# Routing in the attention phase: logits with the gate stationary, transposed back for two batches, and a table of steps for the choice and the places

## The chip, the cores and the metric

The kernel runs on one core of one Trainium2 chip. Time is device microseconds of one execution. The profile is one more execution, with the span of its records and its own time.

## What is computed

32 batches of 256 tokens, width 256, go through cross attention with 16 heads, and then through a mixture of 16 experts of which each token uses four. Of the reference, what matters here:

```python
x = x + xattn(layernorm(x), ctx_1024, ctx_1024, mask, Wq, Wk, Wv, Wo, 16)
# the experts, on layernorm(x):
scores = sigmoid(xt @ gate_w.T)                  # 16 logits a token
_, idx = top_k(scores + gate_b, 4)
w = take_along_axis(scores, idx, axis=-1)
w = w / sum(w, axis=-1, keepdims=True) * 2.5
# y = sum over the four experts of w * expert(xt), plus a shared expert
x = x + y
```

## The kernel before

There are two phases, attention (`emit_attention`) and the experts (`expert_phase`). Attention is one long list of steps, written out for each engine and joined by semaphores. A step `g` is one head of one batch: `b, h = divmod(g, H)` with H = 16, so 512 steps, and a tail to step 520 in which the last pieces end. "Step 6" below means h = 6 in some batch. In every step TensorE makes the scores of head g (L888, L889), a projection of K or Q into one of two `pj` banks (L85 to L87), transposes the probabilities of head g - 3 (L899) and multiplies those of head g - 4 by V (L912). VectorE adds the mask and finds the maximum (L1130), inverts the sums (L1105), adds the halves of the values (L1140; the upper 64 partitions in one step, the lower in the next), writes the low part of Q or K (L1097) and of the probabilities (L1149). float32 products are made of high and low parts, three matmuls each.

Other work shares the `pj` banks at fixed steps: V at steps 4, 5, 12, 13; the output projection at 14, 0, 6, 8; the transposes of x at 9 and of the normed rows at 2 (`rT`). The dictionary `uses` lists what fills a bank in which step. TensorE waits in `bank` until VectorE has emptied the use two before (`s_pjfree`), and every engine takes its part in the order of its own program. So work of VectorE that stands ahead of a low part holds up the bank two uses later.

Routing lies between. For batch b - 2, in step 7, `lg` makes the logits: the transposed rows `xrT` (high and low part) are stationary, the gate with its high and low half is the moving operand of 32 columns, eight matmuls for two tiles of 128 tokens (L837). VectorE sums the halves into `r_sc` (L1064). A set is two batches. In the 15 steps behind the second one's logits `Router.choose` runs one piece k a step: k = 0, 1 the sigmoid (L225, L229), 2 the bias (L231), 3 and 4 the largest values (L235), 5 and 6 their indices (L239), 7 a cast (L242), 8 the one-hot (L244), 9 and 10 halves and mask (L248, L250), 11 the product of one-hot and scores and its reduce (L253, L256), 12 to 14 the weights. A set's pieces thus begin in step 9 of an odd batch and end in step 7 of the next. Three groups of 14, 10 and 8 batches have their rows sorted by expert. For the first two, TensorE counts ranks (`rk`, step 10 of batches 16 and 26, L271 to L278), and `Router.place` turns them into places in the next 18 or 16 steps, with a product and a reduce (L327, L331) for every four tiles. GpSimd then scatters rows by indirect DMA, one every 1.5 steps. It also scales the probabilities (L792) and makes the low parts of the attention (L741) and of the context, the latter in step 3 (L736).

```python
    SET_FROM = [(SET_BATCHES * s + SET_BATCHES + 1) * H + LG_STEP + 1 for s in range(SETS - 1)]
```

```python
                for t, start in enumerate(SET_FROM):
                    if start < g <= start + router.SET_STEPS:
                        router.choose(dve, t, g - start - 1)
```

## Time and profile before

| what | value |
|---|---|
| median of 3 runs | 2213.93 us (2211.66 to 2216.16) |
| the profiled execution's own time | 2211.4 us |
| its span | 2209.6 us |
| ScalarE and GpSimd busy, share of the span | 76% and 63% |
| HBM traffic over the span | 129 GB/s |

Busy time is a sum over instructions; the windows below cut it into stretches. TensorE's records overlap, so in attention a busy share near 100% can still hide waits of about 0.1 us; the start of one matmul to the start of the next shows them. The batches of attention do the same matmuls, apart from logits and ranks, so their lengths can be compared.

### The profile page before, as it was taken

The numbers are of one execution on the slowest core, as the hardware profiler recorded it, in microseconds if no ns is written. First come the engines' busy times: TensorE is split into PE (matmuls) and PEld (weight loads), VectorE is DVE, ScalarE is ACT, GpSimd is POOL, SyncE is SP. The second block draws the span as 40 slices with busy tenths as digits, with TensorE's granted clock in tenths as the row PEclk, the third lists the DMA queues.
The fourth block names the chain that finished last, engine by engine and source line by source line (L and its number), as shares of the span: only waits on it lengthen the run. The fifth ranks groups of instructions, "written<-read, shape, count | busy, mean of one in ns | idle before, by whom it ended". The sixth has DMA issues, their size and how long they took to land. (4 is left out here: it accounts for less than half of the span.)

```text
span 2209.6 us, 57976 instructions
## 1 busy us (share of the span) xinstructions
PE 2086.8 (94%) x16512; PEld 2006.3 (91%) x16512; DVE 1865.4 (84%) x6129; ACT 1677.5 (76%) x4795; POOL 1400.1 (63%) x2094
## 2 busy tenths in 40 slices
PE   7999999999999999999999999999899998898885
PEld 6999999999999998999999998999799998888884
DVE  7999999999999999999999999999764446666687
ACT  6989889888888888898898888889655554454531
POOL 4555655555555555888778877876656646656665
PEclk9999999999999999999999999999999999999997
DMA  7777767777777766866666666666678768887897
GB/s 207 188 182 191 187 175 187 184 181 192 179 187 184 182 168 169 220 188 171 176 180 174 176 167 162 177 172 167 217 254 277 266 240 283 274 283 269 268 331 242
DMA packets 262128, 457.32 MB, mean 207 GB/s; under 512 B 36544, under 2 KB 148672, under 8 KB 261824
## 3 DMA queue, kind: packets, MB, share of 16 engines
q1 hardware_dynamic: 237248, 386.48, 62.8%
q0 software_dynamic: 24576, 67.14, 9.5%
q8 instruction: 148, 2.42, 0.4%
q14 instruction: 156, 1.28, 0.2%
HBM read 141.00 MB, written 144.70 MB: 129 GB/s over the span
## 5 line engine op out<-in xcount | busy, mean ns | idle before, releaser
L792 POOL TENSOR_SCALAR E<-E,rinv 128x256 f32<-128x256 f32 x1024 | 479.6, 479 | 474.8 <-DVE rinv L1105 470.0
L980 ACT ACTIVATE E<-E,negmax 128x256 f32<-128x256 f32 x1024 | 508.9, 502 | 6.8 <-DVE negmax L1130 6.6
L1130 DVE CUSTOM_DVE_ANT_0 E<-pS,m_in 128x256 f32<-128x256 f32 x1024 | 387.5, 416 | 34.4 <-PE pS L889 30.9
L1149 DVE TENSOR_TENSOR PT_lo<-pT,PT_hi 128x512 fp32r<-128x512 f32 x512 | 350.6, 685 | 27.7 <-ACT PT_hi L998 23.6
L1602 POOL DMA_INDIRECT block<-expert_rows,slot x256 | 247.0, 965 | 168.5 <-remote 69.9
L998 ACT ACTIVATE PT_hi<-pT 128x512 fp32r<-128x512 f32 x512 | 304.9, 596 | 9.7 <-PE pT L899 0.5
L899 PE MATMUL pT<-ident,E 128*128 128x128 f32 x2048 | 306.6, 272 | 0.4 <-POOL E L792 0.4
L912 PE MATMUL pV<-PT_hi,V 128*128 128x256 f32 x1024 | 287.2, 303 | 6.1 <-DVE PT_lo L1149 6.0
L964 ACT ACTIVATE qk_sp<-pj 128x256 fp32r<-128x256 f32 x512 | 196.4, 384 | 109.1 <-PE pj L87 95.7
L888 PE MATMUL pS<-qk_st 128*128 128x256 f32 x1024 | 269.1, 284 | 7.8 <-DMA qk_st<-qk_sp 7.6
L889 PE MATMUL pS<-qk_st,qk_sp 128*128 128x256 f32 x1024 | 266.4, 282 | 0.0
L912 PE MATMUL pV<-PT_lo,V 128*128 128x256 f32 x1024 | 265.4, 281 | 0.0
L899 PEld LDWEIGHTS pT<-ident,E 128*128 128x128 f32 x2048 | 235.9, 141 | 0.8 <-POOL E L792 0.6
L1097 DVE TENSOR_TENSOR qk_sp<-pj,qk_sp 128x256 fp32r<-128x256 f32 x512 | 215.0, 420 | 10.6 <-ACT qk_sp L964 2.7
L1140 DVE TENSOR_TENSOR att_sum<-pV,att_sum 64x256 f32<-64x256 f32 x512 | 211.4, 413 | 11.2 <-ACT att_sum L989 1.9
L741 POOL TENSOR_TENSOR att_lo<-att_sum,att_hi 128x256 fp32r<-128x256 f32 x256 | 192.4, 751 | 24.2 <-ACT att_hi L1007 20.5
L912 PEld LDWEIGHTS pV<-PT_hi,V 128*128 128x128 f32 x1024 | 193.9, 189 | 14.3 <-DVE PT_lo L1149 8.6
L989 ACT ACTIVATE att_sum<-pV 64x256 f32<-64x256 f32 x512 | 193.8, 379 | 16.4 <-PE pV L912 4.1
L888 PEld LDWEIGHTS pS<-qk_st 128*128 128x128 f32 x1024 | 195.5, 191 | 10.1 <-DMA qk_st<-qk_sp 9.8
L912 PEld LDWEIGHTS pV<-PT_lo,V 128*128 128x128 f32 x1024 | 194.6, 190 | 6.1
L980 ACT ACTIVATION_READ_ACCUMULATOR E<-E,negmax 128x1 f32 x1024 | 197.9, 193 | 0.0
L889 PEld LDWEIGHTS pS<-qk_st,qk_sp 128*128 128x128 f32 x1024 | 195.7, 191 | 0.1
(265 smaller groups left out, 6879.3 us busy)
## 6 DMA issues: line engine op xcount, KB each, us to landing
qk_st<-qk_sp SPq DMA_DIRECT2D x512, 192.0 KB
qk_st<-qk_sp SPq DMA_DIRECT2D x512, 128.0 KB
sorted_rows<-qk_st SPq DMA_DIRECT2D x152, 256.0 KB, 3.5
xg<-sorted_rows SPq DMA_DIRECT2D x76, 512.0 KB
expert_rows<-block SPq DMA_DIRECT2D x76, 512.0 KB
acc<-x_plus_attention SPq DMA_DIRECT2D x35, 256.0 KB
x_in<-in_x SPq DMA_DIRECT2D x32, 256.0 KB
c_in<-in_ctxT SPq DMA_DIRECT2D x32, 256.0 KB, 4.0
```

The source lines that it names most:

```text
L792: last = pool.tensor_scalar(e[:, t, :], e[:, t, :], rinv[:, r, t:t + 1], 1.0, ALU.mult, ALU.mult)
L888: pe.matmul(pS[g % 2][:, t, :], stacked[:, a, Q_HI, at], stacked[:, a, K_HI, :], start=True, stop=False)
L889: last = pe.matmul(pS[g % 2][:, t, :], plain[:, Q_HI, at], stacked[:, a, K_LO, :], start=False, stop=True)
L899: last = pe.transpose(pT[g % 2][:, k, t * P:(t + 1) * P], e[:, t, k * P:(k + 1) * P], ident[:, :])
L912: last = pe.matmul(pV[g % 2][:, 0:S], V[:, k, j, 2 * a:2 * a + 2, :], PT[g % PT_RING][part][:, k, :], start=k + part == 0, stop=k == NT - ...
L980: last = act.activation(E[r][:, t, :], E[r][:, t, :], ACT.Exp, bias=negmax[:, r, t:t + 1], scale=-1.0, accum_out=rowsum[:, r, t:t + 1])
L998: act.activation(PT[m % PT_RING][0][:, :, :], pT[m % 2][:, :, :], ACT.Copy).then_inc(s_pthi, 1)
L1097: last = dve.tensor_tensor(plain[:, lo, :], ps[:, 0:S], f32(plain[:, hi, :]), ALU.subtract)
L1130: last = dve.tensor_tensor_reduce(out=E[r][:, t, :], in0=pS[g % 2][:, t, :], in1=m_in.tile(b)[:, t, :], scale=-1.0, scalar=BIG, op0=ALU.ad ...
L1140: dve.tensor_tensor(att_sum[pair % 2][half(a), :], pV[n % 2][half(a), 0:S], att_sum[pair % 2][half(a), :], ALU.add).then_inc(s_sum, 1)
L1149: dve.tensor_tensor(lo[:, :, :], pT[n % 2][:, :, :], f32(hi[:, :, :]), ALU.subtract).then_inc(s_ptlo, 1)
L1602: pool.indirect_dma_start(out=cbuf[n % NCB][:, j, :], out_offset=None, in_=expert_rows[g], in_offset=bass.IndirectOffsetOnAxis(ap=shared.s ...
```

## The change

The logits turn round: the gate, repeated four times side by side (4 x 32 = 128 columns), is stationary, and the rows of the batch, 256 tokens, are the moving operand: four matmuls. The result has logits on partitions and tokens along them. VectorE copies for each tile of 128 tokens that quarter of the partitions that belongs to it into `lgT` (the memory of `rowcol`), and once for two batches, in step 8 of the odd ones, TensorE transposes `lgT` (`lt`), and VectorE sums the halves of four tiles at once. For the last batch this is in steps 5 and 7. The exponential on ScalarE comes a step later.

The choice is laid out by the table `CHOICE_AT`, steps from the start of an odd batch. Its piece 11 is split into the product and the reduce (now 12). The places take eight consecutive steps and then those in `QUIET_STEPS`. Where a set's choice would meet the places of a group (sets 7 and 12), it starts a batch later. The start of the scatters follows the last place: 5 steps later for group 0, 4 for group 1. `before` and `done` of the router take the memory of `scan[0]` and `over`.

```diff
-    SET_STEPS = 15
+    SET_STEPS = 16
...
-    SET_FROM = [(SET_BATCHES * s + SET_BATCHES + 1) * H + LG_STEP + 1 for s in range(SETS - 1)]
+    SET_FROM = [(SET_BATCHES * s + SET_BATCHES + 1) * H + LT_STEP + 1 for s in range(SETS - 1)]
...
+    CHOICE_AT = {10: (0,), 11: (1,), 13: (2, 3), 14: (4,), 15: (5, 6), 17: (7, 8), 19: (11,), 21: (9,), 22: (10,), 23: (12, 13), 24: (14, 15)}
+    QUIET_STEPS = (9, 11, 13, 15, 16, 17, 19, 20, 21, 23)
+
+    def place_offsets(c):
+        return [*range(1, router.PLACE_STEPS + 1), *QUIET_STEPS][:router.place_steps(c)]
+
+    def choice_start(s):
+        at = (SET_BATCHES * s + SET_BATCHES + 1) * H
+        crowded = any(at + min(CHOICE_AT) <= RANKS_AT[c] + place_offsets(c)[-1] and RANKS_AT[c] < at + max(CHOICE_AT)
+                      for c in range(EARLY_GROUPS))
+        return at + H if crowded else at
...
-        step = max(step, RANKS_AT[g] + 1 + router.place_steps(g))
+        step = max(step, RANKS_AT[g] + 1 + place_offsets(g)[-1])
...
+        COPIES = P // (2 * N_EXPERTS)
+        gate = sb("gate_parts", [P, NK, COPIES, 2 * N_EXPERTS], F32R)
...
-                    for t in range(NT):
-                        for k in range(NK):
-                            for part in range(2):
-                                last = pe.matmul(ps[:, t * 2 * N_EXPERTS:(t + 1) * 2 * N_EXPERTS],
-                                                 xrT[part][:, k, t * P:(t + 1) * P], gate[:, k, :],
-                                                 start=k + part == 0, stop=k == NK - 1 and part == 1)
+                    for k in range(NK):
+                        for part in range(2):
+                            last = pe.matmul(ps[:, 0:S], gate[:, k, :, :].rearrange("p c n -> p (c n)"), xrT[part][:, k, :],
+                                             start=k + part == 0, stop=k == NK - 1 and part == 1)
+                elif kind == "lt":
+                    pe.wait_ge(s_pjfree, number[("lg", min((n + 1) * SET_BATCHES, EARLY) - 1)] + 1)
+                    last = pe.transpose(ps[:, 0:P], lgT[:, :], ident[:, :])
...
+                    for t in range(NT):
+                        mine = slice((at * NT + t) * 2 * N_EXPERTS, (at * NT + t + 1) * 2 * N_EXPERTS)
+                        last = dve.tensor_copy(lgT[mine, :], ps[mine, t * P:(t + 1) * P])
+                    last.then_inc(s_pjfree, 1)
+                    return
+                if kind == "lt":
+                    dve.wait_ge(s_pj, number[what] + 1)
+                    tiles = min(SET_BATCHES, EARLY - n * SET_BATCHES) * NT
+                    dve.reduce_sum(router.sc[n % 2][:, 0:tiles, :],
+                                   ps[:, 0:tiles * 2 * N_EXPERTS].rearrange("p (t i e) -> p t e i", t=tiles, i=2), AXX).then_inc(s_pjfree, 1)
...
-                for t, start in enumerate(SET_FROM):
-                    if start < g <= start + router.SET_STEPS:
-                        router.choose(dve, t, g - start - 1)
+                for t in range(SETS - 1):
+                    for k in CHOICE_AT.get(g - choice_start(t), ()):
+                        router.choose(dve, t, k)
                 for c in range(EARLY_GROUPS):
-                    if RANKS_AT[c] < g <= RANKS_AT[c] + router.place_steps(c):
+                    if g - RANKS_AT[c] in place_offsets(c):
```

TensorE in step 7 of batch 3, from the transposes of the probabilities to the values, before:

```order
L899 MATMUL pT<-ident,E 128x128 x4
L837 MATMUL pj<-gate_parts,xrT_hi 128x32
L837 MATMUL pj<-gate_parts,xrT_lo 128x32
L837 MATMUL pj<-gate_parts,xrT_hi 128x32
L837 MATMUL pj<-gate_parts,xrT_lo 128x32
L837 MATMUL pj<-gate_parts,xrT_hi 128x32
L837 MATMUL pj<-gate_parts,xrT_lo 128x32
L837 MATMUL pj<-gate_parts,xrT_hi 128x32
L837 MATMUL pj<-gate_parts,xrT_lo 128x32
L912 MATMUL pV<-PT_hi,V 128x256
L912 MATMUL pV<-PT_lo,V 128x256
```

and now (L856 is the logits line, L920 and L933 are the old L899 and L912):

```order
L920 MATMUL pT<-ident,E 128x128 x4
L856 MATMUL pj<-xrT_hi,gate_parts 128x256
L856 MATMUL pj<-xrT_lo,gate_parts 128x256
L856 MATMUL pj<-xrT_hi,gate_parts 128x256
L856 MATMUL pj<-xrT_lo,gate_parts 128x256
L933 MATMUL pV<-PT_hi,V 128x256
L933 MATMUL pV<-PT_lo,V 128x256
L933 MATMUL pV<-PT_hi,V 128x256
```

Eight matmuls of 32 columns have become four of 256.

VectorE from step 7 into step 9 of batch 3, from the low part of Q (L1097; L1128 now) on, before:

```order
L1097 TENSOR_TENSOR qk_sp<-pj,qk_sp 128x256
L1149 TENSOR_TENSOR PT_lo<-pT,PT_hi 128x512
L1064 TENSOR_REDUCE r_sc<-pj 128x32
L1130 ISA E,negmax<-pS,m_in 128x256
...
L1149 TENSOR_TENSOR PT_lo<-pT,PT_hi 128x512
L1078 TENSOR_TENSOR x_in<-pj,x_in 128x256
L1043 TENSOR_SCALAR rows<-x_in,mv,rstd 128x256
L1130 ISA E,negmax<-pS,m_in 128x256
```

and now (L1180 is the old L1149, L1161 the old L1130, L1090 the copies into `rowcol`, L1096 the reduce of the transpose back):

```order
L1128 TENSOR_TENSOR qk_sp<-pj,qk_sp 128x256
L1180 TENSOR_TENSOR PT_lo<-pT,PT_hi 128x512
L1090 COPY rowcol<-pj 32x128 x2
L1161 ISA E,negmax<-pS,m_in 128x256
...
L1128 TENSOR_TENSOR qk_sp<-pj,qk_sp 128x256
L1180 TENSOR_TENSOR PT_lo<-pT,PT_hi 128x512
L1109 TENSOR_TENSOR x_in<-pj,x_in 128x256
L1096 TENSOR_REDUCE r_sc<-pj 128x64
L1065 TENSOR_SCALAR rows<-x_in,mv,rstd 128x256
L1161 ISA E,negmax<-pS,m_in 128x256
```

The reduce of step 7 has become two copies, and a reduce of four tiles stands in step 8 between the output projection's add and the norm.

VectorE from step 3 to step 5 of batch 4, choice of set 0, before:

```order
L1149 TENSOR_TENSOR PT_lo<-pT,PT_hi 128x512
L250 TENSOR_TENSOR r_mask<-r_halves 128x64
L1130 ISA E,negmax<-pS,m_in 128x256
...
L1149 TENSOR_TENSOR PT_lo<-pT,PT_hi 128x512
L1093 TENSOR_TENSOR V<-pj,V 128x4x128
L1035 BN_AGGR mv<-st 128x2 x2
L253 TENSOR_TENSOR r_prod<-r_onehot,r_sc 128x256
L256 TENSOR_REDUCE r_taken<-r_prod 128x16
L1130 ISA E,negmax<-pS,m_in 128x256
```

and now:

```order
L1180 TENSOR_TENSOR PT_lo<-pT,PT_hi 128x512
L253 TENSOR_TENSOR r_prod<-r_onehot,r_sc 128x256
L1161 ISA E,negmax<-pS,m_in 128x256
...
L1180 TENSOR_TENSOR PT_lo<-pT,PT_hi 128x512
L1124 TENSOR_TENSOR V<-pj,V 128x4x128
L1057 BN_AGGR mv<-st 128x2 x2
L1161 ISA E,negmax<-pS,m_in 128x256
```

The product L253 has moved up to the end of step 3, ahead of the maxima of step 4; the mask (L250) and the reduce (L256) are gone from here to steps 6 and 7.

## Rows read from the trace of the kernel before

**Rows 1.** The page, part 1: busy us, share of the span, instructions.

```profile
PE 2086.8 (94%) x16512; PEld 2006.3 (91%) x16512; DVE 1865.4 (84%) x6129; ACT 1677.5 (76%) x4795; POOL 1400.1 (63%) x2094
```

**Rows 2.** Busy time of five stretches from 159.68 to 1509.41 us: their sum.

```profile
sum 1349.73, PE 1333.27 PEld 1289.20 DVE 1270.08 ACT 1186.42 POOL 905.07; mean PE 266.65 PEld 257.84 DVE 254.02 ACT 237.28 POOL 181.01
```

**Rows 3.** Stretches of batches 2, 8, 9, 17: us, busy by engine, PEclk.

```profile
112.91:159.68 46.77, 46.77 (x378) 45.68 (x377) 43.03 (x150) 41.88 (x127) 26.88 (x49) 1.00 0.74 187
...
397.00:444.59 47.59, 47.36 (x378) 45.90 (x377) 44.88 (x163) 42.30 (x127) 27.16 (x49) 1.00 0.74 184
444.59:491.83 47.24, 47.11 (x379) 45.79 (x378) 44.10 (x161) 42.17 (x128) 26.66 (x49) 1.00 0.74 185
827.57:880.74 53.17, 49.26 (x379) 46.32 (x377) 51.85 (x190) 43.47 (x128) 26.71 (x48) 1.00 0.67 169
```

**Rows 4.** Timeline of TensorE, batch 8: start, us, line, [idle before].

```profile
405.54 0.28 PE L889 MATMUL pS<-qk_st,qk_sp 128*128 128x256 f32 x1
405.75 0.38 PE L85 MATMUL pj<-xnT_hi,wq_hi 128*128 128x256 f32 x1
405.97 0.28 PE L86 MATMUL pj<-xnT_lo,wq_hi 128*128 128x256 f32 x1
...
415.45 0.39 PE L85 MATMUL pj<-cT_hi,wk_hi 128*128 128x256 f32 x1 [0.23 <-DVE qk_sp L1097]
```

**Rows 5.** The same, batch 16, step 10: ranks, then values.

```profile
808.73 0.35 PE L271 MATMUL pj<-r_mask,tri 128*128 128x448 bf16 x1
...
812.25 0.36 PE L912 MATMUL pV<-PT_hi,V 128*128 128x256 f32 x1
```

**Rows 6.** The same, batch 9, step 7: first logits matmul, then values.

```profile
466.97 0.26 PE L837 MATMUL pj<-gate_parts,xrT_hi 128*128 128x32 f32 x1
...
467.87 0.36 PE L912 MATMUL pV<-PT_hi,V 128*128 128x256 f32 x1
468.07 0.28 PE L912 MATMUL pV<-PT_lo,V 128*128 128x256 f32 x1
468.18 0.28 PE L912 MATMUL pV<-PT_hi,V 128*128 128x256 f32 x1
```

**Rows 7.** The same, batch 9, step 2: two lots of four transposes.

```profile
451.43 0.60 PE L899 MATMUL pT<-ident,E 128*128 128x128 f32 x4
451.87 0.60 PE L828 MATMUL pj<-ident,rows 128*128 128x128 f32 x4
```

**Rows 8.** Groups by form, VectorE, 397 to 873 us: busy, mean ns, idle.

```profile
L229 DVE RECIPROCAL r_sc<-r_sc 128x64 f32<-128x64 f32 x5 | 2.7, 535 | 0.0
...
L1064 DVE TENSOR_REDUCE r_sc<-pj 128x32 f32<-128x64 f32 x10 | 2.1, 214 | 0.0
...
L256 DVE TENSOR_REDUCE r_taken<-r_prod 128x16 f32<-128x256 f32 x5 | 2.1, 420 | 0.2
```

**Rows 9.** Timeline of VectorE, batch 9, steps 3 and 4: reciprocal, sum, low part.

```profile
455.08 0.16 DVE L1105 RECIPROCAL rinv<-rowsum 128x2 f32<-128x2 f32 x1
455.15 0.40 DVE L1140 TENSOR_TENSOR att_sum<-pV,att_sum 64x256 f32<-64x256 f32 x1
455.48 0.41 DVE L1097 TENSOR_TENSOR qk_sp<-pj,qk_sp 128x256 fp32r<-128x256 f32 x1
...
457.22 0.17 DVE L1105 RECIPROCAL rinv<-rowsum 128x2 f32<-128x2 f32 x1
457.41 0.43 DVE L1140 TENSOR_TENSOR att_sum<-pV,att_sum 64x256 f32<-64x256 f32 x1
457.87 0.42 DVE L1097 TENSOR_TENSOR qk_sp<-pj,qk_sp 128x256 fp32r<-128x256 f32 x1
```

**Rows 10.** GpSimd and VectorE in batch 8; then all products.

```profile
411.97 1.29 POOL L736 TENSOR_TENSOR cT_lo<-c_in,cT_hi 128x512 fp32r<-128x512 f32 x1
...
412.40 1.14 DVE L253 TENSOR_TENSOR r_prod<-r_onehot,r_sc 128x256 f32<-128x256 bf16 x1
...
L253 DVE TENSOR_TENSOR r_prod<-r_onehot,r_sc x16: 426/1134/1492, 222.3 to 1611.7; 128x256 f32<-128x256 bf16 x16
```

More of the change, by code:

```diff
@@ L188, in __init__ @@
         self.scan = [sb(f"scan{n}", [P, N_EXPERTS]) for n in range(2)]
-        self.before = sb("before", [P, N_EXPERTS])
-        self.done, self.passed = sb("done", [P, N_EXPERTS]), sb("passed", [P, 1])
+        self.before = self.scan[0]
+        self.done, self.passed = self.over, sb("passed", [P, 1])
         self.s_exp, self.s_mask = sem("exp"), sem("mask")
@@ L496, in emit_attention @@
         sv = Ring(sb, sem, "sv", 2, [P, NT, D], F32)
-        gate = sb("gate_parts", [P, NK, 2 * N_EXPERTS], F32R)
+        COPIES = P // (2 * N_EXPERTS)
+        gate = sb("gate_parts", [P, NK, COPIES, 2 * N_EXPERTS], F32R)
         rowcol = sb("rowcol", [P, P])
+        lgT = rowcol
+        assert COPIES == SET_TILES
         st62, mv2 = sb("st62", [P, NT, 6]), sb("mv2", [P, NT, 2])
@@ L547, in emit_attention @@
                 use(g, ("rT", b - 2))
-            if h == LG_STEP and 0 <= b - 2 < EARLY:
+            ends = b - 2 == EARLY - 1
+            if 0 <= b - 2 < EARLY and h == LG_STEP - (END_STEPS if ends else 0):
                 use(g, ("lg", b - 2))
+            if 0 <= b - 2 < EARLY and h == LT_STEP - (END_STEPS - 1 if ends else 0) and ((b - 2) % SET_BATCHES == SET_BATCHES - 1 or ends):
+                use(g, ("lt", (b - 2) // SET_BATCHES))
             for c in range(EARLY_GROUPS):
@@ L941, in hi_part @@
                 kind, n = what[0], what[1]
-                if kind in ("wo", "lg", "rk"):
+                if kind in ("wo", "lg", "lt", "rk"):
                     return
@@ L1009, in _ @@
                     act.wait_ge(shared.s_gate, 3 * DMA)
-                    act.activation(gate[:, :, 0:N_EXPERTS], shared.gate[:, :, :], ACT.Copy).then_inc(s_gatehi, 1)
+                    act.activation(gate[:, :, :, 0:N_EXPERTS], shared.gate[:, :, :].unsqueeze(2).broadcast_to([P, NK, COPIES, N_EXPERTS]),
+                                   ACT.Copy).then_inc(s_gatehi, 1)
                 if g == SHARED_STEP:
@@ L1018, in _ @@
                     t = SET_FROM.index(g)
-                    act.wait_ge(s_pjfree, number[("lg", SET_BATCHES * (t + 1) - 1)] + 1)
+                    act.wait_ge(s_pjfree, number[("lt", t)] + 1)
                     router.exponentials(act, t)
@@ L1062, in lo_part @@
                     dve.wait_ge(s_pj, number[what] + 1)
-                    logits, at = n // SET_BATCHES, n % SET_BATCHES * NT
-                    scores = dve.reduce_sum(router.sc[logits % 2][:, at:at + NT, :],
-                                            ps[:, 0:NT * 2 * N_EXPERTS].rearrange("p (t i e) -> p t e i", t=NT, i=2), AXX)
-                    scores.then_inc(s_pjfree, 1)
+                    turn, at = divmod(n, SET_BATCHES)
+                    if at == 0 and turn:
+                        dve.wait_ge(s_pj, number[("lt", turn - 1)] + 1)
+                    for t in range(NT):
[8 more added lines that the diff above has]
+                                   ps[:, 0:tiles * 2 * N_EXPERTS].rearrange("p (t i e) -> p t e i", t=tiles, i=2), AXX).then_inc(s_pjfree, 1)
                     return
@@ L1167, in _ @@
                     dve.wait_ge(s_gatehi, 1)
-                    dve.tensor_tensor(gate[:, :, N_EXPERTS:2 * N_EXPERTS], shared.gate[:, :, :], f32(gate[:, :, 0:N_EXPERTS]),
-                                      ALU.subtract).then_inc(s_gatelo, 1)
+                    for k in range(NK):
+                        last = dve.tensor_tensor(gate[:, k, :, N_EXPERTS:2 * N_EXPERTS],
+                                                 shared.gate[:, k, :].unsqueeze(1).broadcast_to([P, COPIES, N_EXPERTS]),
+                                                 f32(gate[:, k, :, 0:N_EXPERTS]), ALU.subtract)
+                    last.then_inc(s_gatelo, 1)
                     dve.wait_ge(s_iota, 2)
```

11 lines of the change are left out of this document (6 added, 5 removed).

## The prediction

> **What bounds the kernel now.** The page comes first: TensorE is busy for 94% of the span, VectorE for 84% [rows 1]. Those are averages over two phases, so the next view is the busy time in stretches cut at a batch's first score matmul. In batches 3 to 30 TensorE is busy for 1333.3 of 1349.7 us, VectorE for 1270.1 [rows 2]. Attention is bound by TensorE, with VectorE close behind. A busy row hides short waits, since a matmul is shown for 0.28 us and the next starts 0.12 after it; so compare lengths of batches that do the same matmuls. Batch 2, before any routing, takes 46.77 us; the granted clock is 1.00 there and in all that follow. With routing an even batch takes 47.59 and an odd one 47.24, and batch 17, which holds the places of group 0, takes 53.17 [rows 3]. The excess over 46.77 is TensorE waiting for VectorE: in step 6 of batch 8 the projection of K starts after 0.23 us in which nothing at all ran, released by VectorE's low part of Q [rows 4].
>
> All 28 batches at 46.77 would be 1309.6 us; they take 1349.7, so 40.1 is excess. The 14 plain sets hold 14 x (0.82 + 0.47 us) = 18.1. The rank matmuls of group 0 delay the values by 3.6 us (812.25 less 808.73, and 0.1 for the change of shape) [rows 5]; by 40 matmuls against 56, group 1 has about 2.5. That leaves 40.1 - 18.1 - 6.1, about 16 us, for the places of the two groups, which fall on top of the choices.
>
> **Logits on TensorE.** Now there are eight matmuls of 32 columns, each with a weight load: the first starts at 466.97 and the values follow at 467.87, so 0.90 us, 0.11 each, bound by the loads [rows 6]. The change has four of 256 columns. The values of that form start 0.12 apart (468.18 less 468.07; the first interval, 0.20, holds 0.08 for the change of shape, which is there either way) [rows 6]: 4 x 0.12 = 0.48. Saved: about 0.42, taken as 0.41, x 31 batches = 12.7 us. Added: one transpose for two batches, 16 in all. Four transposes of that form take 0.44 [rows 7], so 0.11 each, 1.8 us. Net 10.9 us, all of it on the engine that bounds attention.
>
> **Logits on VectorE.** A reduce of 0.21 us per batch goes (31 x) [rows 8]. Two copies of 32 partitions x 128 elements come, and per set one reduce of 128. No row shows the copy. A 64-element read of PSUM takes 0.21 [rows 8], 256 elements 0.41 [rows 9]; between them 128 elements give 0.28. How close they can follow each other is seen in the sums of attention: in steps where the 64-partition add works on the upper half, it starts 0.19 after the reciprocal and the next instruction 0.46 after it; on the lower half 0.07 and 0.33 [rows 9]. So crossing to other partitions costs 0.12 on each side. Of the two copies the second always starts at other partitions than the first, hence no overlap: 0.56 to 0.68 for the pair. The low bound is 2 x 0.21, the high one 2 x 1.49, the longest that any routed instruction was held [rows 10]; I take 0.6, nearest to the rows of the same kind. Per set: 2 x 0.6 + 0.28 - 2 x 0.21 = +1.05 us.
> The Trainium skill (VectorE: DVE Perf Modes, Two Vector instructions with no wait between them) states this as a rule: an instruction whose first input or output starts in another group of 32 partitions than the last one's is held until all before it are finished. Without it the pair would be 0.42 and VectorE's sum 0.7 us per set better.
> Who covers this? Step 7 of TensorE is 2.99 long and becomes 2.58; VectorE idles 3.74 us in a batch without routing [rows 3]. In even batches the copies share step 7 with a reduce of 0.42 [rows 8], which leaves VectorE about 0.5 us late; steps 8 and 0 to 6 have longer work on TensorE. I cost it at nothing. If that cover goes, it is 1.05 x 15.5 = 16 us.
> The third use in step 8 of odd batches (the transpose back) makes the bank of the next K that of the output projection. VectorE's add there ends about half a us before TensorE asks; nothing.
>
> **The product moves from step 4 to step 3.** At 412.40 the product of one-hot and scores takes 1.14 us. GpSimd works on the low part of the context from 411.97 for 1.29, to 413.26, and the product ends 0.28 after that; the same line takes 0.43 at its shortest, with no such neighbour [rows 10]. So 0.7 us of each product is waiting for GpSimd. With the reduce behind it (0.42 [rows 8], less an overlap of 0.1) step 4 carries 1.5 us of choice, and step 6 pays with the gap [rows 4]. In the change step 4 has none, step 3 the product alone, where GpSimd has not begun with the context; the reduce goes to step 7. That removes the waits of steps 4 to 6, the 0.63 of the 0.82 that the wait in step 3 doesn't explain. What stays is the wait at step 3, behind the one-hot in step 1: in step 3 the projection of Q starts 0.21 after the matmul before it and its next 0.22 later, 0.19 more than 0.12 each (405.75 and 405.97) [rows 4]. It grows by 0.07, the cast now beside it: even batches go from 0.82 to 0.26.
> The Trainium skill (SBUF — State Buffer, two separate sides) has a rule that fits: VectorE with two SBUF inputs and GpSimd share a port pair, and the later one blocks fully. The trace agrees (1.14 against 0.43). By it the product would be held again wherever it meets GpSimd, which is a rival below.
> **Odd batches.** Ahead of step 12's projection there were the reciprocal (0.54) and two small operations of 64 elements, now one of these; at 0.21 less the overlap [rows 8] it is worth 0.13. The excess 0.47 goes to about 0.34. Nothing stands in steps 9, 12 and 0; two FIND_INDEX pairs share step 15, and step 0 of TensorE (3.5 us) absorbs that.
> A set now costs 0.26 + 0.34 = 0.60 instead of 1.29: 14 x 0.69 = 9.7 us.
>
> **Places.** Their 18 and 16 pieces keep their work; a middle piece is a product and a reduce, 0.43 + 0.42 less the overlap, about 0.8 us. Before, they stood in consecutive steps, one of them held by GpSimd, with the choice of the same two batches on top. Now the light steps 9 to 11 still take three in a row, about 2.4 us more than TensorE gives there. Counting what VectorE falls behind against the 1.2 us that two banks let it: about 0.2 + 0.8 (steps 3 to 5), 2.7 (steps 9 to 13), 0.6 behind the rows, so 4.3 for group 0 and 3.5 for group 1. 16 less 7.8 is 8.2; I take 8.6, as the shorter logits step also falls there. The choice of sets 7 and 12 moves one batch on and keeps its 0.60. Scatters on GpSimd's queue start 5 and 4 steps later at the two groups; the number of batches scattered in attention stays 18, and the last still falls 6 steps before the end. Gate copies in batch 1 are once, under 1 us. The expert phase gets the same choice in the same eight units: nothing.
>
> **Sum.** 10.9 + 9.7 + 8.6 = 29.2 us. The profiled execution took 2211.4 (its span is 2209.6) and would take 2182.2; the median of the three runs shown, 2213.93, is 2.5 above it and becomes 2184.7. A measurement of this kernel can tell 0.2%, 4.4 us.
>
> **Rivals.**
> 1. *VectorE becomes the bound.* It was busy 44.88 of 47.59 in even batches [rows 3], and TensorE's 0.41 is taken from just the step where the copies arrive. Against it: 2.7 us of idleness remain. Then the 10.9 us are not seen: 2195.6.
> 2. *The port again.* The product in step 3 meets GpSimd after all, or the halves in step 5 do. VectorE would be 0.7 late at step 4; with 1.0 from steps 1 to 3 that is 0.5 over what two banks allow: 0.6 x 14 = 8.4, so 2193.1.
> 3. *The waits only move.* The table is as crowded as the old rule and neither sets nor groups gain: 2213.9 - 10.9 = 2203.0. Against it is that a known 0.7 per set vanishes.
> 4. *Slower.* The copies are held as the product was. At 1.49 each [rows 10] a step 7 of VectorE is 2.1 + 3.0 against 2.58: 2.5 late, 1.3 beyond what the banks allow, in 31 batches 40 us: 2225. The gain of 29.2 is eaten from 0.94 us a batch, that is from about 1.3 us per copy. Against it: they read PSUM, not two SBUF operands, and the 0.21 reduce never waited.
> 5. *No effect*, the gate form costing what it saves: 2213.9. *All waits of sets and groups gone*: 2213.9 - 10.9 - 34 = 2169.
>
> **Chances.** Forecast 0.70, rivals in order 0.08, 0.08, 0.05, 0.04, no effect 0.02, all gone 0.03. The sizes that I am least sure of are the group term (4 us either way) and the sets (4 us), so the forecast reaches from 2175 to 2194; with rivals 1 to 3 the range is 2175 to 2203. Faster by over 0.2%: 0.94; within: 0.02; slower: 0.04.
>
> **What would show it.** Right: batches 8 and 9 at about 46.6 and 46.8 us (46.77 - 0.41, + 0.11 for the transpose, + 0.26 or 0.34); the product at 0.43; copies near 0.28; batch 17 under 51; no wait for VectorE in steps 4 to 6. Wrong: a product still above 1 us, VectorE late in step 8, or a batch length that has not shrunk in step 7.

## The result, and the profile after

The changed kernel takes 2201.45 us (median of five runs, 2199.9 to 2203.5), the kernel before 2213.93 over the same five rounds: ratio 0.9948, 95% interval 0.9934 to 0.9963, so 12.5 us faster. The forecast was 2184.7, 29.2 us. The profiled execution's span is 2199.6 us.

The page of the changed kernel, part 1 (beside [rows 1]):

```profile
PE 2073.7 (94%) x16404; PEld 1991.0 (91%) x16404; DVE 1873.9 (85%) x6177; ACT 1681.9 (76%) x4795; POOL 1399.5 (64%) x2094
```

TensorE has 13.1 us less work, VectorE 8.5 us more. Stretches of batches 2, 8, 9, 10, 11, 17, 19 and 29 of the changed kernel (columns as in [rows 3]), then the sum over batches 3 to 30, which answers to [rows 2]:

```profile
114.08:160.71 46.63, 46.53 (x374) 45.23 (x374) 43.37 (x151) 42.03 (x127) 26.89 (x49) 1.00 0.81 191
396.47:444.32 47.85, 47.41 (x375) 45.47 (x374) 45.43 (x168) 42.36 (x127) 27.26 (x50) 1.00 0.78 183
444.32:491.43 47.11, 46.87 (x376) 45.45 (x375) 44.41 (x159) 42.26 (x128) 26.43 (x48) 1.00 0.78 185
491.43:538.58 47.15, 46.98 (x374) 45.44 (x374) 44.94 (x168) 42.26 (x127) 27.17 (x50) 1.00 0.78 186
538.58:585.51 46.93, 46.70 (x375) 45.38 (x375) 44.35 (x159) 42.27 (x128) 26.46 (x48) 1.00 0.78 186
823.86:874.57 50.71, 48.43 (x375) 45.72 (x375) 48.83 (x170) 43.24 (x128) 26.06 (x48) 1.00 0.73 177
923.06:972.97 49.91, 48.14 (x375) 45.70 (x375) 47.70 (x176) 42.92 (x128) 37.87 (x59) 1.00 0.70 181
1406.83:1455.91 49.08, 48.03 (x376) 45.66 (x375) 47.48 (x176) 43.10 (x128) 40.05 (x60) 1.00 0.65 170
...
sum 1342.50, PE 1324.97 PEld 1277.00 DVE 1277.13 ACT 1189.98 POOL 900.16; mean PE 264.99 PEld 255.40 DVE 255.43 ACT 238.00 POOL 180.03
```

Batches 3 to 30 fell by 7.2 us (1349.73 to 1342.50). Plain batches are those without ranks, places and delayed choices; undisturbed ones have no wait for a transfer either. These are 47.05 and 46.92 us long (even and odd, batches 12 and 13; forecast 46.6 and 46.8). Batch 17 lost 2.5 us, but 19 and 29, which hold the delayed choices, gained 2.3 and 1.8. The rest of the 12.5 us lies outside these batches.

The pieces cost what the forecast said. TensorE in batch 10, step 7 (start, us), from the first logits matmul to the values after it, 0.56 us instead of 0.90 [rows 6]:

```profile
514.37 0.36 PE L856 MATMUL pj<-xrT_hi,gate_parts 128*128 128x256 f32 x1
514.57 0.28 PE L856 MATMUL pj<-xrT_lo,gate_parts 128*128 128x256 f32 x1
514.69 0.28 PE L856 MATMUL pj<-xrT_hi,gate_parts 128*128 128x256 f32 x1
514.81 0.28 PE L856 MATMUL pj<-xrT_lo,gate_parts 128*128 128x256 f32 x1
514.93 0.28 PE L933 MATMUL pV<-PT_hi,V 128*128 128x256 f32 x1
```

VectorE's groups by line in batches 3 to 30 (busy, mean ns, idle before): the copies of the logits, the wide reduce, the product.

```profile
L1090 DVE COPY rowcol<-pj 32x128 f32<-32x128 f32 x56 | 15.9, 285 | 0.8
...
L253 DVE TENSOR_TENSOR r_prod<-r_onehot,r_sc 128x256 f32<-128x256 bf16 x14 | 5.7, 407 | 0.0
L1096 DVE TENSOR_REDUCE r_sc<-pj 128x64 f32<-128x128 f32 x14 | 4.0, 285 | 0.0
```

And VectorE's timeline where the copies stand, batch 10:

```profile
515.28 0.69 DVE L1180 TENSOR_TENSOR PT_lo<-pT,PT_hi 128x512 fp32r<-128x512 f32 x1 [0.23 <-ACT PT_hi L1019]
515.89 0.57 DVE L1090 COPY rowcol<-pj 32x128 f32<-32x128 f32 x2
516.49 0.42 DVE L256 TENSOR_REDUCE r_taken<-r_prod 128x16 f32<-128x256 f32 x1
516.94 0.17 DVE L258 TENSOR_REDUCE r_wsum<-r_taken 128x4 f32<-128x16 f32 x1
517.14 0.42 DVE L1161 CUSTOM_DVE_ANT_0 E<-pS,m_in 128x256 f32<-128x256 f32 x1
```

The pair of copies takes 0.60 us to the next start. Step 7 of TensorE runs from 512.83 to 515.40, so the copies begin only after it, and what follows runs beside step 8. The idle 0.23 us ahead of the low part in the first row is the last idle time that the view shows for VectorE until after step 8.

How late VectorE is can be read from its first maximum of a step. In step 8 of batch 10 it came 0.68 us after TensorE's first score matmul before the change, and VectorE had idled ahead of it (before):

```profile
516.48 0.28 PE L888 MATMUL pS<-qk_st 128*128 128x256 f32 x1
...
517.16 0.43 DVE L1130 CUSTOM_DVE_ANT_0 E<-pS,m_in 128x256 f32<-128x256 f32 x1 [0.31 <-PE pS L889]
```

Now the matmul starts as below and the maximum at 517.14, so 1.74 us after it (after):

```profile
515.40 0.28 PE L909 MATMUL pS<-qk_st 128*128 128x256 f32 x1
```

0.68 us is the least that any step has, so VectorE is 1.06 us late. The six even batches from 4 to 14 all show 1.74 (to 0.01).

### The profile page after: what moved, and what is told of

It reads as the page before. It is cut to its first block and busy times, and to the rows that moved or that the text cites. A ratio compares the mean times of both kernels' runs of the same rounds, so it can differ in the third digit from the quotient of the medians.

```text
span 2199.6 us, 57839 instructions
## 1 busy us (share of the span) xinstructions
PE 2073.7 (94%) x16404; PEld 1991.0 (91%) x16404; DVE 1873.9 (85%) x6177; ACT 1681.9 (76%) x4795; POOL 1399.5 (64%) x2094
## 5 line engine op out<-in xcount | busy, mean ns | idle before, releaser
L1161 DVE CUSTOM_DVE_ANT_0 E<-pS,m_in 128x256 f32<-128x256 f32 x1024 | 386.6, 414 | 18.7 <-PE pS L910 16.3
L1180 DVE TENSOR_TENSOR PT_lo<-pT,PT_hi 128x512 fp32r<-128x512 f32 x512 | 350.0, 684 | 23.8 <-ACT PT_hi L1019 20.0
L920 PE MATMUL pT<-ident,E 128*128 128x128 f32 x2048 | 307.9, 273 | 0.5 <-POOL E L812 0.5
L933 PE MATMUL pV<-PT_hi,V 128*128 128x256 f32 x1024 | 286.1, 301 | 5.3 <-DVE PT_lo L1180 5.3
L933 PE MATMUL pV<-PT_lo,V 128*128 128x256 f32 x1024 | 266.2, 282 | 0.0
L920 PEld LDWEIGHTS pT<-ident,E 128*128 128x128 f32 x2048 | 237.9, 141 | 0.9 <-POOL E L812 0.8
L1128 DVE TENSOR_TENSOR qk_sp<-pj,qk_sp 128x256 fp32r<-128x256 f32 x512 | 214.5, 419 | 11.7 <-ACT qk_sp L985 3.7
L933 PEld LDWEIGHTS pV<-PT_hi,V 128*128 128x128 f32 x1024 | 194.4, 190 | 15.6 <-DVE PT_lo L1180 8.9
L933 PEld LDWEIGHTS pV<-PT_lo,V 128*128 128x128 f32 x1024 | 195.1, 191 | 5.6
L1801 ACT ACTIVATE block<-epY 128x512 f32<-128x512 f32 x152 | 91.3, 601 | 136.7 <-PE epY L87 87.7
```

The source lines that it names most:

```text
L920: last = pe.transpose(pT[g % 2][:, k, t * P:(t + 1) * P], e[:, t, k * P:(k + 1) * P], ident[:, :])
L933: last = pe.matmul(pV[g % 2][:, 0:S], V[:, k, j, 2 * a:2 * a + 2, :], PT[g % PT_RING][part][:, k, :], start=k + part == 0, stop=k == NT - ...
L1128: last = dve.tensor_tensor(plain[:, lo, :], ps[:, 0:S], f32(plain[:, hi, :]), ALU.subtract)
L1161: last = dve.tensor_tensor_reduce(out=E[r][:, t, :], in0=pS[g % 2][:, t, :], in1=m_in.tile(b)[:, t, :], scale=-1.0, scalar=BIG, op0=ALU.ad ...
L1180: dve.tensor_tensor(lo[:, :, :], pT[n % 2][:, :, :], f32(hi[:, :, :]), ALU.subtract).then_inc(s_ptlo, 1)
```

## Where the time stands, step by step

For every kernel of the study I took, from the trace, the length of each of the 448 steps of batches 3 to 30 (first score matmul to first score matmul) and subtracted the shortest of the same step in that kernel. Sums in us ("bare" is 28 times the shortest steps):

```
                             bare   excess by step of the batch                total
                                     3    6    8    9   10   11   13  others
before (E9)                 1307.9  5.0  8.4  1.4  0.1  7.4  3.7  6.6   8.1    1348.6
after (E5)                  1294.1  9.4  0.0  2.9  3.0  9.2  8.3  9.1   5.8    1341.8
table only (E2)             1305.8  9.6  1.7  0.1  0.0  5.7  6.9  5.3   8.0    1343.1
copies on ScalarE (E6)      1294.2  9.5  0.1  0.9  1.7  6.5  3.9  9.2   6.4    1332.4
E6, table after lag (E10)   1294.2  2.7  1.8  4.0  1.5  7.3  8.7  2.9   8.0    1331.1
E10, x later (E18)          1294.4  2.8  0.5  4.2  1.5  7.3  4.3  3.3   6.7    1324.9
copies twice (E15)          1300.7  8.8  0.1  5.8  8.7 11.1  5.7  9.5   6.6    1357.0
```

This table is the centre of the case. The change took 13.8 us off the bare steps and emptied step 6 (8.4), but put 13.1 into steps 3, 8, 9, 10 and 13, where TensorE waits for VectorE, and step 11 rose by 4.6. The excess of all steps is 40.7 us before, 37.3 with the table only, 47.7 after, and 38.2 with the copies on ScalarE. So, added to the table, the new logits took 11.7 us off the bare steps and brought 10.4 us of waits.

Step 11 rose for two reasons. In undisturbed plain even batches it is 2.31 us instead of 2.10, a wait for VectorE that goes when the copies do (2.09 in E6). And in some batches TensorE waits for transfers of `qk_st`, the Q and K of a pair of heads, which SyncE's queue moves there from `qk_sp`: in E5 all 2.9 us of these waits stand at the first score matmul of a step 12, and so lengthen step 11; in E9 0.8 do. TensorE's waits in attention, of before (E9) and after (E5) on further chips (us, times, longest):

```profile
PE pj L85 <- DVE qk_sp L1097: 10.3, 22, 0.9
PE pS L888 <- DMA qk_st<-qk_sp: 2.6, 5, 1.0
PE pV L912 <- DVE PT_lo L1149: 1.8, 2, 1.0
```

```profile
PE pj L85 <- DVE qk_sp L1128: 12.3, 36, 0.8
PE pS L909 <- DMA qk_st<-qk_sp: 2.9, 5, 1.1
PE pV L933 <- DVE PT_lo L1180: 0.9, 2, 0.5
PE pj L860 <- DVE qk_sp L1128: 0.9, 2, 0.5
```

The view of waits shows only gaps in which the engine is empty; the step lengths show the rest.

## Experiments

The chips differ: the kernel before took 2125.5 to 2126.0 us on three (E1 to E4, E5 to E8, E12 to E15), 2201.9 and 2210.8 on two others (E9 to E11, E16 to E18). Batches 3 to 30 of the changed kernel took 1341.8 and 1342.5 us on a chip of either kind, and what follows attention some 80 us more on the second. So ratios to the kernel before, from the same chip, are compared, or times of one chip. Theory A: the work that the logits put on VectorE makes the waits. Theory B: the table's places make them. Each median is of 4 to 12 executions, but for E9, which was executed once for its trace. The numbers in brackets are 95% intervals.

**E1, the logits alone** (places and choices in consecutive steps):

```
-CHOICE_AT = {10: (0,), 11: (1,), 13: (2, 3), ... 24: (14, 15)}
+CHOICE_AT = {10: (0,), 11: (1, 2), 12: (3,), 13: (4,), ... 20: (11, 12), 21: (13,), 22: (14,), 23: (15,)}
-QUIET_STEPS = (9, 11, 13, 15, 16, 17, 19, 20, 21, 23)
+QUIET_STEPS = tuple(range(9, 19))
-        return at + H if crowded else at
+        return at
```

> The new logits (four wide matmuls, copies, transpose back) with the choices and places in consecutive steps as before; product and reduce again together in step 4 of the even batch. Theory A (the work that the logits add on VectorE, 1.05 us per set, makes TensorE wait, and eats part of its saving of 10.9 us): 2205 to 2209. Theory B (the copies lie under cover, and what was lost against the forecast is lost by the table of steps): the full 10.9 us, 2203 or a little under, with steps 9 to 11 of an even batch as long as before (2.54, 2.10, 2.10).

Measured 0.9992 [0.9984, 1.0001]: of 10.9 us hardly 2 arrive. Even plain batches do get the whole 0.41 (47.57 to 47.14) and steps 9 to 11 stay as they were, for B. But odd ones stay at 47.23: step 13 rose from 3.93 to 4.37, as I read it since the transpose back starts each set a step later and I had put two operations into step 11. Some 4 us of that (0.32 x 14, against 4.05 in the changed kernel) are then my edit's; 4.6 us more are in step 11, where this profile has as many us of waits for transfers, and the rest at the groups, where step 8 of batches 17 and 27 takes 5.27 and 5.65 us.

**E2, the table alone** (logits as before).

> The table of steps for choices and places, with the logits as before. Theory A: without the copies the table keeps what I forecast for sets and groups, 18.3 us, so 2196 to 2199, and steps 10 and 11 of an even batch are 2.10 again. Theory B (the table puts its load where VectorE is late already: one-hot and cast in step 1, the first two pieces in steps 10 and 11 of odd batches): step 3 of an even batch still about 2.5 and step 13 of an odd one about 4.0 us; it gains the 0.65 of step 6 and part of the groups and loses 0.3 a set, 2203 to 2208.

0.9947 [0.9934, 0.9960], as the whole change: on top of the table the new logits gain nothing. Both theories hold a part: even step 3 is 2.53 (it was 2.29), step 13 is 3.89, and steps 8 to 10 are clean (3.54, 2.54, 2.10), where the change has its new waits. In plain batches these need both halves; at the groups E1 has them too. A plain set fell from 94.8 us to 94.2 (47.13 and 47.09), so the table alone brought 0.6 of the 0.69 us that I had forecast for it.

**E3, no delay of sets 7 and 12** (`return at`, nothing else).

> The changed kernel, but the choices of sets 7 and 12 are not put one batch later. If the delay is worth what it was made for, the group of places again falls on a choice and the kernel is 2 to 4 us slower than the changed one (2203 to 2206). If the delay costs as much as it saves (batches 19 and 29 are 2.8 and 1.9 us longer than a plain odd batch in it, 4.7 in all), it comes out the same, 2200 to 2203, with the waits in batches 17, 18, 27 and 28.

0.9977 [0.9966, 0.9988] beside 0.9956 for the changed kernel in E5 and 0.9948 in the first comparison, both on other chips, so 4 to 6 us slower; the interval overlaps E5's by 0.0003. The delay pays, though batches 19 and 29 carry its cost: batches 17 to 19 and 27 to 29 are 6.6 us longer together than in E5, 2.6 of it one wait for a transfer in batch 19.

**E4, the product in step 4 again** (`19: (11,)` becomes `20: (11,)`).

> The changed kernel with the product of one-hot and scores one step later, step 4 of the even batch, where it stood before; the reduce stays in step 7. If the port was the cause of the wait in step 6, the product takes about 1.1 us again; without the reduce behind it VectorE is 0.4 less late than before, so step 6 waits 0.2 to 0.5 us, x 14: 3 to 7 us slower than the changed kernel, less 0.1 a set that step 5 may save. If it was only the sum of product and reduce, the product takes 0.41 and nothing is lost: 2201.

0.9974 [0.9966, 0.9983]. Group of the product in this run:

```profile
L253 DVE TENSOR_TENSOR r_prod<-r_onehot,r_sc 128x256 f32<-128x256 bf16 x14 | 16.0, 1141 | 0.0
```

So the product is held again (1141 ns, against 407), yet the plain batches are 47.04 and 46.92 as in the changed kernel, and step 6 is 3.53. Without the reduce behind it, the held product costs TensorE nothing in these batches. The kernel is some 4 us slower than E5; batches 3 to 30 are 2.4 us longer, and against the first trace of the changed kernel batches 24 and 30 are 1.2 us longer each, mostly in step 8 (4.33 for 3.53), among the scatters. In plain batches the wait of step 6 was the sum of the two, and splitting them was enough.

**E5, the changed kernel again**, for a trace and a ratio on a chip like that of E1 to E4 (the kernel before takes 2125.5 us there, 2125.8 on theirs).

> The changed kernel itself, unaltered, beside the other runs. On this chip the kernel before takes 2125.8 us (its attention is as before, its experts are some 85 us shorter). Attention is the same work, so the changed kernel should be 10 to 13 us faster again: 2113 to 2116. If the waits for a qk_st transfer that differ from run to run (1.8 to 5.4 us in a profile) make up the differences of single profiles, the steps of plain batches are the same to 0.02 us and only those waits differ.

0.9956 [0.9943, 0.9969]. Plain batches agree with the first trace to 0.02 us; single steps 11 do not (3.37 in batch 7, where it was 2.12).

**E6, the copies on ScalarE**: the two copies move into its queue, VectorE reads one element to hand the bank back.

```
-                        last = dve.tensor_copy(lgT[mine, :], ps[mine, t * P:(t + 1) * P])
+                        last = act.activation(lgT[mine, :], ps[mine, t * P:(t + 1) * P], ACT.Copy)
...
+                    dve.wait_ge(s_lg, n + 1)
+                    dve.tensor_copy(lg_done[:, :], ps[:, 0:1]).then_inc(s_pjfree, 1)
```

> The changed kernel with the two copies of the logits on ScalarE, and one 1-element read on VectorE to hand the bank back. Table and transpose stay. Theory A (the copies on VectorE bring the waits in steps 10 and 11 of even batches, 0.32, and in step 8 and 9 at the groups): those waits go, even batches 46.75 and batches 17, 19, 27, 29 shorter by 0.5 to 1 each, so 6 to 8 us faster than the changed kernel. Rival: ScalarE, busy 80% of the time, is late in step 7 and its copies push the exponentials: waits of the same size for ScalarE, no gain or a loss.

0.9918 [0.9905, 0.9931]: 7.6 us faster than the changed kernel on this chip (2108.72 against 2116.3). The groups of both copies, on ScalarE and what VectorE keeps:

```profile
L974 ACT ACTIVATE rowcol<-pj 32x128 f32<-32x128 f32 x56 | 14.8, 265 | 0.7
```

```profile
L1096 DVE COPY r_passed<-pj 128x1 f32<-128x1 f32 x28 | 4.3, 152 | 0.0
```

The 0.32 us of steps 10 and 11 go in every undisturbed plain even batch (46.72), and steps 8 to 10 lose 6.0 us in all. The maximum of step 8 of batch 10 comes 1.12 us after TensorE's matmul instead of 1.74, that of step 10 1.12 instead of 1.55. ScalarE has room.

**E7, another table**, and **E8, E7 with E6's copies**:

```
+CHOICE_AT = {12: (0, 1), 13: (2, 3), 14: (4,), 15: (5, 6), 20: (7,), 21: (8, 11), 22: (9, 10, 12), 23: (13,), 24: (14, 15)}
```

> The changed kernel with another table for the choices: the first two steps at 12 instead of 10 and 11, one-hot and product together in step 5 of the even batch (after GpSimd has the context), nothing in steps 0 to 3, cast 4, halves, mask and reduce 6, sum 7, weights 8. Theory B (what is left of the set's waits is where its steps stand against the lag that two banks allow): step 3 of even batches back to 2.10 and step 13 of odd ones to 3.50, steps 10 and 11 to 2.10 or 2.15; 0.43 + 0.55 + 0.2 = 1.2 us a set, x 14, so 13 to 17 us faster than the changed kernel. Theory A (the amount of VectorE's work, not its place, makes the waits): they turn up in steps 7 to 9 instead, gain under 4 us.

> Both: copies on ScalarE and the new table. If each takes away waits of its own, the gains add except in steps 10 and 11, which both empty: 16 to 20 us under the changed kernel. If the copies no longer matter once steps 6 to 9 hold less, as the new table alone.

0.9953 and 0.9954: nothing for E7, and E8 loses what E6 had. The waits of step 3 and most of step 13 (4.05 to 3.64) go, but step 8 of even batches rises from 3.53 to 4.1, and to 5.3 among the scatters. VectorE in batch 22 of E7:

```profile
1087.49 0.42 DVE L1109 TENSOR_TENSOR x_in<-pj,x_in 128x256 f32<-128x256 f32 x1
1087.82 0.88 DVE L1065 TENSOR_SCALAR rows<-x_in,mv,rstd 128x256 f32<-128x256 f32 x1
1088.62 0.76 DVE L248 TENSOR_TENSOR r_halves<-r_onehot 128x128 bf16<-128x128 bf16 x1
1089.42 0.19 DVE L250 TENSOR_TENSOR r_mask<-r_halves 128x64 bf16<-128x64 bf16 x1
1089.53 0.41 DVE L256 TENSOR_REDUCE r_taken<-r_prod 128x16 f32<-128x256 f32 x1
```

and GpSimd beside it:

```profile
1087.46 1.05 POOL L791 DMA_INDIRECT sorted_rows<-sv,slot  x1 [0.16 <-issue]
1088.54 0.75 POOL L761 TENSOR_TENSOR att_lo<-att_sum,att_hi 128x256 fp32r<-128x256 f32 x1
```

Step 6 holds five operations behind each other. Beside the scatter the norm (L1065) takes 0.88 us (0.47 on the mean), and beside the low part of the attention the halves (L248) take 0.76 (0.22 in batches without such a neighbour). Both forecasts of 13 us and more missed: place decides, and I had filled one step too much.

**E9, the kernel before again; E10, a table fitted to the lag; E11, E10 with the places moved too.** For E10 I measured how long after the start of the next step VectorE ends each low part of K or Q, and put operations where that leaves room. E10 and E11 also have the copies on ScalarE. E11 adds the second line.

```
+CHOICE_AT = {12: (0, 1), 13: (2, 3), 14: (4,), 15: (5, 6), 20: (7,), 21: (8, 11), 22: (9,), 23: (10, 12), 24: (13, 14, 15)}
+PLACE_AT = (2, 2, 3, 3, 3, 5, 5, 5, 11, 12, 14, 18, 19, 20, 21, 27, 28, 28)
```

> The kernel before, unaltered, for its trace on this chip. Plain batches 47.57 and 47.24 as on the other chip; the stretch of batches 3 to 30 at 1349.7 plus what qk_st transfers add here (1 us there). If those waits belong to the faster kernels, it has 1 us of them; if to this chip, 3 to 6.

> Copies on ScalarE, first and second step of a set at 12, cast 4, one-hot and product 5 of the even batch as in the new table, but in step 6 the halves alone, mask and reduce in 7, the last three in 8. If step 8 of the even batch waited (0.58, up to 1.8 among the scatters) because step 6 held rows, halves, mask and reduce, these waits go: even batches 46.3 to 46.4, odd 46.5, so 0.8 us a set under the run with the copies on ScalarE alone, 8 to 12 us: 2097 to 2101. If VectorE's amount decides, the waits show in steps 8 to 10 and nothing is gained, 2108.

> The same with the places of the two early groups in other steps: the eight light operations in steps 12, 13 and 15, the middle pieces only in steps 5, 6, 8 and 12 to 15, the end in steps 5 and 6; scatters start 5 steps later. Batches 17 and 27 fall from 49.9 and 51.6 to about 47.5 and 48.5, so 4 to 6 us less than the run before. Rival: the scatters, later, collide with the end of attention and the expert phase starts later by what was gained.

In E9 plain batches are 47.57 and 47.24, as expected, with 2.6 us of waits for transfers, between the 1 and the 3 to 6 of the two readings. E10 0.9919 [0.9906, 0.9933], E11 0.9935 [0.9921, 0.9949]. In E10 undisturbed batches are 46.43 and 46.51, shorter by 0.7 a set, as planned, but the time is that of E6. The table of steps above shows why: steps 3 and 13 lost 13.1 us against E6, but step 11 gained 4.8, step 8 3.0 (most of it in batches 24 and 30, among the scatters) and step 6 1.6 (one wait for a transfer in batch 19). E10's waits, its transfers on SyncE's queue in batch 13, and TensorE there:

```profile
PE pj L85 <- DVE qk_sp L1133: 6.4, 11, 1.0
PE pS L910 <- DMA qk_st<-qk_sp: 5.0, 8, 1.8
```

```profile
652.59 1.74 SPq L651 DMA_DIRECT2D qk_st<-qk_sp  x1
654.38 0.60 SPq L652 DMA_DIRECT2D qk_st<-qk_sp  x1
655.02 0.62 SPq L665 DMA_DIRECT2D sorted_rows<-qk_st  x1
655.68 0.61 SPq L657 DMA_DIRECT2D x_plus_attention<-x_in  x1
656.39 1.03 SPq L616 DMA_DIRECT2D x_in<-in_x  x1
657.64 0.62 SPq L651 DMA_DIRECT2D qk_st<-qk_sp  x1
658.31 0.62 SPq L652 DMA_DIRECT2D qk_st<-qk_sp  x1
658.98 0.62 SPq L651 DMA_DIRECT2D qk_st<-qk_sp  x1
659.64 1.36 SPq L652 DMA_DIRECT2D qk_st<-qk_sp  x1
```

```profile
663.10 0.39 PE L910 MATMUL pS<-qk_st 128*128 128x256 f32 x1 [0.81 <-DMA qk_st<-qk_sp]
```

Three transfers of 256 KB (a clearing, the store and the load of x) are issued just ahead of the pair whose transfers follow step 9. Its scores are those of step 12, and the wait for it is counted in step 11, which it lengthens (some expectations below put it as the transfers that step 11 needs). Steps 10 and 11 last 2.1 us each, the shortest two in a row, so this pair has the least time of the batch. E11 had 9.3 us of these waits, one of 2.3; whether its places are better can't be read from it.

**E12 to E14, the clearings moved** away from the pairs of steps 1 and 9: on the changed kernel, on E6 and on E10.

```
-                        if 0 <= what[1] - FIRST_CLEAR < len(clear_after):
-                            clear_sorted(*clear_after[what[1] - FIRST_CLEAR])
+                        for _ in range((2, 1, 0, 1)[what[1] % 4] if what[1] >= FIRST_CLEAR else 0):
+                            if cleared[0] < len(clear_after):
+                                clear_sorted(*clear_after[cleared[0]])
+                                cleared[0] += 1
```

> The changed kernel; of the clearings of 256 KB that follow a pair's transfers, none any more behind the pairs of steps 1 and 9 (where the loads of context and mask, and the store and load of x, stand too), two instead behind those of steps 5 and 13. If the waits for qk_st come from that pile, they fall from 1.8 to 2.9 us to under 1 and the kernel is 1 to 3 us faster than the changed one (ratio to before 0.9935 to 0.995). If they come from the transfers' own phase, the same as the changed kernel (0.995), or worse, with the waits in steps 7 and 15.

> The copies on ScalarE and the clearings moved. If transfers are the next bound: ratio 0.989 to 0.991, 2 to 4 us better than the copies on ScalarE alone (0.9918), waits for qk_st under 1 us. Otherwise 0.992.

> Copies on ScalarE, the table fitted to the lag, and the clearings moved. With the waits for qk_st at 5.0 us in the same without the last part, theory of the transfers: 3 to 5 us of them go, and with them what they hid, ratio 0.9875 to 0.990 (0.9919 without). Otherwise 0.992.

0.9965 [0.9953, 0.9978], 0.9926 [0.9913, 0.9939] and 0.9921 [0.9905, 0.9936], with 3.5, 3.0 and 7.9 us of waits for qk_st: a miss. The clearing that stands ahead of x in the rows above is not among those that the edit moved (it is still there in the trace of E14), so these runs show only that moving the clearings behind the pairs of steps 1 and 9 took no waits away.

**E15, each copy made twice** on VectorE.

```
+                        dve.tensor_copy(ps[mine, S + t * P:S + (t + 1) * P], ps[mine, t * P:(t + 1) * P])
                         last = dve.tensor_copy(lgT[mine, :], ps[mine, t * P:(t + 1) * P])
```

> The changed kernel with each of the two copies made twice on VectorE (the extra one into the unused half of the same bank), 0.6 us more VectorE in step 7 of every batch. Theory A (VectorE's work in step 7 of even batches has no cover left): even batches 0.5 to 0.6 longer, the groups and the batches with scatters too, odd plain batches 0 to 0.1: 8 to 12 us slower than the changed kernel, ratio about 1.000. If it is covered: 0.995 as the changed kernel.

1.0040 [1.0025, 1.0054] beside E5's 0.9956, 17.9 us slower than the changed kernel, for 31 x 0.57 = 17.7 us more of VectorE. Even plain batches grew by 0.65 and odd ones by 0.62, which I had put at nothing: there too steps 8 and 9 now wait. No cover is left for more work in step 7.

**E16 to E18, store and load of x four steps later**: on the changed kernel, on E6 and on E10.

```
-                if h == WO_STEPS[-1] - H and b:
+                if h == WO_STEPS[-1] - H + (4 if b < B else 0) and b:
```

> The changed kernel with the store of x plus attention and the load of x issued in step 12 instead of 8. If they hold up the transfers that step 11 needs, these waits (1.8 to 3.5 us) go and 1 to 3 us are gained, ratio 0.994 to 0.995. If not, 0.9956 or a little over and the waits stand where they stood, or in step 15.

> The copies on ScalarE and x in step 12. Without the last part 0.9918 to 0.9926. If the pile is the bound, 0.990 to 0.9915; otherwise the same.

> Copies on ScalarE, the table fitted to the lag, x in step 12. Without the last part 0.9919 with 5.0 us of waits for qk_st. If the pile is the bound these fall under 1.5 us and the table's gain shows in the time: 0.988 to 0.990. If the waits come back elsewhere (step 15 or 3), 0.992, and the transfers are late for another reason.

0.9944 [0.9930, 0.9957], 0.9906 [0.9891, 0.9921] and 0.9875 [0.9860, 0.9890]. Waits for qk_st are 0.5, 1.2 and 2.1 us (2.9, 1.3 and 5.0 in E5, E6 and E10). At the first score matmul of step 12, where the edit should help, none is left in E16 and E17 and one in E18 (0.75 us in batch 22; E10 had seven, 3.2 us); the others stand elsewhere, most in step 6 of batch 19. E16 and E17 gain about 0.1%, within the intervals; E18 gains 0.4%, some 9 us, with an interval apart from E10's; of that the trace shows 6.2 us in batches 3 to 30 (4.4 in step 11) and 2.9 in the first three, where two profiles of the changed kernel differ by 2.0. E18's waits:

```profile
PE pj L85 <- DVE qk_sp L1133: 6.3, 12, 1.0
PE pS L910 <- DMA qk_st<-qk_sp: 2.1, 3, 1.1
```

Its batches 9, 11, 13 and 15 are all 46.51 to 46.53. E17 and E18 ran on one chip and differ by the table alone: 2190.6 and 2183.1 us, so the table fitted to the lag is worth 7.4 us once x is out of the way. E18 is the best version of the study: 2183.1 us beside 2210.8, 27.7 us faster than the kernel before.

## Why the forecast was wrong

The direction was right, the size was not: 12.5 for 29.2 us. 2201.45 us lies above the 2175 to 2194 of the forecast proper, and within the wider range to 2203 only because that took in rivals. Of the 16.7 us that are missing, E6 gives back 7.6 by moving the copies off VectorE; the rest is in the sets and the places. Point by point:

- **Logits on TensorE**, 10.9 us: right. Step 7 went from 2.99 to 2.58 in every batch. The transpose back costs 0.11 an odd batch (3.56 and 2.62 for 3.53 and 2.54).
- **Logits on VectorE, costed at nothing**: this step failed. The durations were right (285 ns a copy, 0.60 a pair). The second copy starts 0.28 or 0.30 us after the first, 0.01 behind its end, where the norm behind x's add in step 8 of batch 10 starts 0.08 ahead of that add's end. The Trainium skill (VectorE: DVE Perf Modes, Two Vector instructions with no wait between them) states that a change of partition group holds an instruction until those before it have finished, and the trace agrees. (That a set would be 0.7 us better with a pair of 0.42 was wrong: 2 x (0.60 - 0.42) is 0.36. Nothing was built on it.)

  The cover was read wrongly. I had VectorE about 0.5 us late after step 7; it is 1.06, mostly since I left out the sum beside the reduce (0.20) and 0.23 in which VectorE waited for ScalarE. I counted VectorE's idleness over a batch, 3.74 us, and took step 8 onwards as room; but step 8 gives back only 0.27, and steps 9 to 11 are among the shortest. In step 10 of batch 10 the maximum comes 1.55 us after the matmul and in step 11 1.93, and TensorE waits 0.11 and 0.21; before the change and in E6 it is 1.12 and 1.63, and TensorE doesn't wait. In odd batches there is no reduce in step 7, the maximum of step 8 comes after 1.23, and the copies cost nothing.

  E6 prices the copies at 7.6 us, and E15 shows that as much work again costs 17.9; my own figure for lost cover was 16.
- **The product moved**, even excess 0.82 to 0.26: it came to 47.04 less the 46.28 of a batch without a choice (batch 2), both in E5, so 0.76. Step 6 did lose its wait, and the product runs at 407 ns. But E4 shows that in plain batches GpSimd's hold alone cost nothing; product and reduce together did. The Trainium skill (SBUF — State Buffer, two separate sides) states that a VectorE operation with two SBUF inputs and a GpSimd operation lock each other out of a port pair that they share. The trace agrees: 1141 ns beside GpSimd's work, 407 without. Step 3 grew by 0.24 and not 0.07, since one-hot and cast in step 1 delay it (with them moved, in E7 and E10, it is 2.10); steps 10 and 11 got 0.32 that E2 and E6 do not have.
- **Odd batches**, 0.47 to 0.34: it became 0.53 beside the transpose. E2, without copies and transpose back, has 3.89 in step 13; the change and E6 have 4.05, so the 0.16 goes with the transpose. A set costs 1.29 as before: the 9.7 us did not come. Per set, 0.32 of the 0.69 is the copies' (E6), 0.17 is step 3, and the rest step 13.
- **Places**, 8.6 us: over plain batches the ten batches 16 to 20 and 26 to 30 held 21.2 us in E9 and 22.5 in E5. Batch 17 gained as forecast (50.71), but "keeps its 0.60" failed: the delayed sets make batches 19 and 29 of E5 1.6 and 2.2 us longer than plain ones, and against E6 the copies add 0.25 to 0.8 in step 8 of batches 17, 19, 27 and 29 and 0.2 to 0.4 in step 9 of 17, 19 and 29. E3 shows that without the delay it is worse. The 1.2 us that two banks let VectorE fall behind had no row: in step 10 the 0.44 us of before (1.12 less 0.68) cost nothing and the 0.87 of after already make TensorE wait.
- Rival 3, **the waits only move**, gave 2203.0, within 2 us of the result. Its picture of the whole is right: the excess went from 40.7 to 47.7 us. Its division is not, and there the number is luck: it had the logits bring all of their 10.9 us and the table nothing, but the table alone brings as much as the whole (E2) and the logits alone hardly 2 us (E1). That part is rival 1, VectorE as the bound where the copies stand. I gave rival 3 0.05, because "a known 0.7 per set vanishes". The wait of step 6 did vanish; I had not asked, step by step, how late VectorE already was where the work went.

Open: what sets the transfer's delay in a given batch (the same kernel has it at different batches in two runs), and whether E11's places are better without it. Of the miss at the places the 6 to 7 us that the copies don't explain were not tested one by one. Some 5 of the 12.5 us lie outside batches 3 to 30 and were not taken apart.

## What to carry to other kernels

A bound engine that hands buffers to a nearly full one is not covered by that engine's average idleness: for each step write down how late the helper ends against the next hand-over, and add work only where that leaves room before the next short step. When a table of steps is made from such lags, count the fixed operations of the step first, and expect the next resource (here the transfers of a pair behind 512 KB of others) to show once the waits are gone: the new table showed nothing in E10's time until E18 moved these.
